# Layer 1 of a graph network: one tile in four chunks from TensorE, and weights' matmuls in 64-row pairs

## The reference, cut to what matters

```
h = relu(layernorm(x))
x = x + relu(norm_dst * segment_sum((h * norm_src)[src], dst) @ W + b)           # layer 0
h = relu(layernorm(x))                                                           # 8 scalars, 8 vectors of 3
w = relu(edge_attr_32 @ W1 + b1) @ W2 + b2      # (edges, 4, 8, 8): a weight matrix set per edge
m0 = a * ((s[src]*sh0) . w_000 + c * (v[src].sh1) . w_110)
m1 = a * (s[src] sh1 . w_011 + (v[src]*sh0) . w_101)
x = x + [segment_sum(m0) + s @ si_w0, segment_sum(m1) + v @ si_w1]               # layer 1
```

## Time and profile before

| | us |
|---|---|
| median of 3 runs | 4124.31 (4122.82 to 4134.66) |
| the profiled execution | 4122.98, span 4121.1 |
| busy: PE, PEld | 3132.6 (76%), 2298.3 (56%) |
| busy: VectorE, ScalarE | 2649.4 (64%), 1693.6 (41%) |
| busy: GpSimd | 3087.7 (75%) |
| chain of waits | GpSimd 59%, issue 24%, VectorE 8%, PE 3% |
| DMA | mean 29 GB/s |

### The profile page before, as it was taken

How to read it: one execution, slowest core, us unless ns; L and a number is a source line. 1 busy time by engine, 2 the same in 40 slices (tenths; PEclk the granted TensorE clock), 3 DMA queues, 4 the chain that set the end, 5 groups by cost and what they waited for, 6 DMA issues and landing times.

```text
span 4121.1 us, 82454 instructions
## 1 busy us (share of the span) xinstructions
PE 3132.6 (76%) x20394; PEld 2298.3 (56%) x20395; DVE 2649.4 (64%) x5843; ACT 1693.6 (41%) x5935; POOL 3087.7 (75%) x3210
## 2 busy tenths in 40 slices
PE   5654444468777777777788888888888888888887
PEld 4544444444444443343466667666677667666676
DVE  8995444455555554454577777777777777777776
ACT  3210000013333333333655555555555555555554
POOL 7767777777777777777677777777777777777775
PEclk9996555568888888988899999999999999999999
DMA  2021111111111111111111111111111111111111
GB/s 56 14 54 39 38 38 38 38 27 23 22 23 23 22 23 22 21 22 21 26 30 28 28 28 29 30 28 28 29 30 29 28 28 29 30 28 28 29 30 18
DMA packets 244961, 119.57 MB, mean 29 GB/s; under 512 B 148880, under 2 KB 226065, under 8 KB 244817
## 3 DMA queue, kind: packets, MB, share of 16 engines
q0 software_dynamic: 102528, 52.70, 9.1%
q1 hardware_dynamic: 131625, 48.99, 5.1%
q10 hardware_dynamic: 10768, 17.44, 1.3%
HBM read 113.94 MB, written 4.92 MB: 29 GB/s over the span
## 4 chain that ended last, share of the span: by engine, by line
POOL 59%; issue 24%; DVE 8%; PE 3%; DMA 1%; DVEq 1%; ACT 1%; POOLq 1%; ACTq 0%; SPq 0%
POOL g L447 59%; DVE acc_b L952 4%; DMA g<-table,idx 1%; PE ps L704 1%; PE ps L738 1%; PE ps L772 1%; ACT onehot L579 1%; DVEq L952 0%; ACT onehot L586 0%; DVE hn L1212 0%; DVE prod_a L1066 0%; DVE ef L1195 0%; ACT root L557 0%; DVE stat L905 0%; DVE stat L902 0%
## 5 line engine op out<-in xcount | busy, mean ns | idle before, releaser
L447 POOL DMA_INDIRECT g<-table,idx x2980 | 2872.1, 964 | 935.1 <-issue 902.5
L828 PE MATMUL ps<-w_s,hid 128*128 128x256 f32 x3328 | 884.8, 417 | 270.0 <-ACT hid L627 220.8
L828 PEld LDWEIGHTS ps<-w_s,hid 128*128 128x128 f32 x3328 | 660.4, 207 | 437.5 <-DVE prod_a L1270 231.3
L579 ACT ACTIVATE onehot<-iota_all,dst_rel 128x68 f32<-128x68 f32 x2648 | 673.8, 337 | 384.4 <-DVEq L1132 319.8
L639 ACT ACTIVATE q<-g,sh 128x32 f32<-128x32 f32 x1664 | 375.4, 308 | 861.5 <-DMA g<-table,idx 861.5
L738 PE MATMUL ps<-split_s,prod_a 128*128 128x512 bf16 x1736 | 572.7, 415 | 34.4 <-DVE prod_a L1057 33.5
L1275 DVE TENSOR_REDUCE msg_b<-prod_b 128x128 f32<-128x1024 f32 x416 | 502.1, 1207 | 0.0
L704 PE MATMUL ps<-onehot,g 128*33 128x68 f32 x2880 | 269.4, 263 | 273.8 <-issue 173.8
L1245 DVE TENSOR_TENSOR vsh<-g,sh 128x192 f32<-128x192 f32 x208 | 81.7, 393 | 580.1 <-ACT q L642 580.1
L704 PEld LDWEIGHTS ps<-onehot,prod_a 128*128 128x128 f32 x3328 | 388.8, 192 | 86.1 <-issue 86.0
L704 PEld LDWEIGHTS ps<-onehot,g 128*33 128x33 f32 x2880 | 233.4, 137 | 344.1 <-issue 327.5
(11 more groups left out here) (132 smaller groups left out, 3437.3 us busy)
## 6 DMA issues: line engine op xcount, KB each, us to landing
g<-table,idx POOLq DMA_INDIRECT x2980
ef<-edge_t SPq DMA_DIRECT2D x208, 128.0 KB
ef<-src_rows ACTq DMA_DIRECT2D x27, 512.0 KB, 3.6
prod_a<-src_rows SPq DMA_DIRECT2D x124, 64.0 KB, 3.0
idx<-src_chunks SPq DMA_DIRECT2D x416, 4.0 KB
g<-x_rows,idx POOLq DMA_INDIRECT x224
sh<-sh_chunks SPq DMA_DIRECT2D x208, 16.0 KB
table<-hn ACTq DMA_DIRECT2D x5, 320.0 KB, 3.5
```

The source lines that it names most:

```text
L447: pool.indirect_dma_start(out=g[:, j, t, 0:FEAT], out_offset=None, in_=table, in_offset=bass.IndirectOffsetOnAxis(ap=idx[:, j, t:t + 1], a ...
L579: ins = act.activation(onehot[:, b, t, :], iota_all[:, 0:WIN], ACT.Square, scale=-1.0, bias=dst_rel[:, bass.ds(c * TILES + t, 1)])
L828: mm = pe.matmul(w_ps[h][:, t, :], hid[:, h, P * t:P * t + P], w2_s[:, :], start=True, stop=True)
```

## The change

Layer 1 now takes tile 7 of the chunk at position 3 (ROWS_AT) of each iteration from 2 (ROWS_FROM) on from TensorE: GpSimd gathers seven tiles there. `table2` is read back in 7 groups by SP, into two stages, and split by VectorE in three bf16 parts (`split_group`), one group after each of the chunks 0 to 6. The sources of the tile are loaded into `keys2`, VectorE makes the selection at the end of step 3 (`make_source2`), TensorE multiplies in step 0 behind the window sums (`source_rows2`), VectorE chooses at the end of step 1 (`choose2`). Iterations 0 and 1 are unrolled.

Weights: both halves of `hid` lie in one buffer, half 0 in rows 0 to 63 and half 1 in rows 64 to 127, and W2 is there twice. `weights` makes both halves at once: four bf16 matmuls (32-row groups) write the bias, held as three bf16 parts in the first rows of each group of 32, into the four banks, and then the eight weight matmuls follow, half 0 and half 1 in turn, in 64-row groups, adding to it. It waits for both halves of the chunk before to be used. `hidden` writes both halves into the bank H_BANK, on partitions 0 to 63 and 64 to 127. The bank next to it takes the table's rows. ScalarE's two clears of `hid` go; a bias row is loaded and scaled, split and masked by 14 linked operations of VectorE before `weights_scaled`. SP loads three DMAs more at the start. Blocks of the output are added in `x`, not in `xc`.

```diff
--- before.py
+++ after.py
+            load_group(0)
+            load_group(1)
+            load_key2(RING * ROWS_FROM + ROWS_AT)
...
                                  load_from(sh_chunks, c + RING)).then_inc(sh_in[j], 16)
+                    if isinstance(c, int) and c + 2 < GROUPS:
+                        sp.wait_ge(split2_done, c + 1)
+                        load_group(c + 2)
+                    if j == 0 and rows_made_in(i):
+                        load_key2(RING * i + (RING + ROWS_AT))
...
                     pool.sem_inc(slots_opened, 1)
-                    for t in range(tiles):
+                    for t in range(MADE if rows_made and j == ROWS_AT else tiles):
                         pool.indirect_dma_start(
...
                 act.wait_ge(hidden_psum, 2 * (RING * i + j) + h + 1)
-                act.activation(hid[0:HID, h, :], ps[0:HID, H_BANK + h, :], ACT.Relu,
-                               bias=b1_s[:, 0:1]).then_inc(hidden_ready, 1)
+                half = slice(HID * h, HID * h + HID)
+                act.activation(hid[half, 0, :], ps[half, H_BANK, :], ACT.Relu,
+                               bias=b1_s[half, 0:1]).then_inc(hidden_ready, 1)
 
...
-                act.wait_ge(gathered[j], landed2(i))
+                act.wait_ge(gathered[j], landed2(i, j))
+                if j == ROWS_AT and rows_made_in(i):
+                    act.wait_ge(row2_made, i - 1)
...
                         row = 64 * (j % 2) + 32 * h
-                        mm = pe.matmul(ps[0:HID, H_BANK + h, at:at + 256], w1_s[row:row + 32, :],
+                        mm = pe.matmul(ps[HID * h:HID * h + HID, H_BANK, at:at + 256], w1_s[row:row + 32, :],
                                        ef[row:row + 32, 512 * (j // 2) + at:512 * (j // 2) + at + 256], start=True,
-                                       stop=True, tile_position=(row, 0))
+                                       stop=True, tile_position=(row, HID * h))
                 mm.then_inc(hidden_psum, 2)
 
-            def weights(i, j, h):
-
-                if beyond(i, j, h):
+            def weights(i, j):
+
+                if beyond(i):
                     return
-                k = 2 * (RING * i + j) + h
-                pe.wait_ge(hidden_ready, k + 1)
-                wait(pe, weights_used, k - 1)
+                k = 2 * (RING * i + j)
+                pe.wait_ge(hidden_ready, k + 2)
+                wait(pe, weights_used, k)
+                for u in range(4):
+                    h, t = u % 2, u // 2 * 2
+                    rows = slice(32 * u, 32 * u + 32)
+                    pe.matmul(w_ps[h][:, t:t + 2, :], ones_b[rows, :], bias_b[rows, :, :], start=True, stop=False,
+                              tile_position=(32 * u, 0), skip_group_check=True)
                 for t in range(4):
-                    mm = pe.matmul(w_ps[h][:, t, :], hid[:, h, P * t:P * t + P], w2_s[:, :], start=True, stop=True)
-                mm.then_inc(weights_ready, 1)
+                    for h in range(2):
+                        rows = slice(HID * h, HID * h + HID)
+                        mm = pe.matmul(w_ps[h][:, t, :], hid[rows, 0, P * t:P * t + P], w2_s[rows, :], start=False,
+                                       stop=True, tile_position=(HID * h, 0), skip_group_check=True)
+                        if t == 3:
+                            mm.then_inc(weights_ready, 1)
+
+            def source_rows2(m):
+
+                pe.wait_ge(split2_done, GROUPS)
+                pe.wait_ge(source2_ready, m + 1)
+                for k in range(GROUPS):
+                    for n in range(3):
+                        mm = pe.matmul(rows2_ps, source2[:, k, :], split[n][:, k, :],
+                                       start=(k == 0 and n == 0), stop=(k == GROUPS - 1 and n == 2))
+                mm.then_inc(rows2_psum, 1)
 
...
                     b = j % 2
-                    weights(*half(i, j, 2))
-                    weights(*half(i, j, 3))
+                    weights(i + (j + 1) // RING, (j + 1) % RING)
                     hidden(i + (j + 2) // RING, (j + 2) % RING)
                     pe.wait_ge(onehot2_ready, c + 1)
                     pe.wait_ge(messages_ready, c + 1)
                     wait(pe, added2, c - 1)
                     window_sums(c, messages_of(b), j, b, seg2_done, 1)
+                    if j == 0 and rows_made_in(i):
+                        source_rows2(i - ROWS_FROM)
                     if j == LOOK:
                         next_block(pe, blocks2, final_blocks(pe, RING * i + (LOOK - 1)), out_block)
 
...
             link(dve.tensor_scalar(w2_s[:, 64:256], w2_s[:, 64:256], float(ALPHA), None, ALU.mult))
+            dve.wait_ge(bias_in, 16)
+            link(dve.memset(ones_b, 1.0))
+            link(dve.tensor_scalar(bias_f[:, 0:64], bias_f[:, 0:64], float(ALPHA * C110), None, ALU.mult))
+            link(dve.tensor_scalar(bias_f[:, 64:256], bias_f[:, 64:256], float(ALPHA), None, ALU.mult))
+            for k in range(3):
+                link(dve.tensor_copy(bias_part, bias_f))
+                if k < 2:
+                    link(dve.tensor_tensor(bias_f, bias_f, bias_part, ALU.subtract))
+                for u in range(2):
+                    if k == 0:
+                        link(dve.tensor_scalar(bias_b[:, u, :], bias_part, masks[:, 0:1], None, ALU.mult))
+                    else:
+                        link(dve.scalar_tensor_tensor(out=bias_b[:, u, :], in0=bias_part, scalar=masks[:, k:k + 1],
+                                                      in1=bias_b[:, u, :], op0=ALU.mult, op1=ALU.add))
             dve.tensor_scalar(sel_b_s[64:96, :], sel_b_s[64:96, :], float(SI_SCALE), None,
                               ALU.mult).then_inc(weights_scaled, 1)
 
 
+            def split_group(k):
+
+                n = group_rows(k)
+                full = stage2[k % 2][0:n, :]
+                high, middle, rest = (part_s[0:n, k, :] for part_s in split)
+                dve.wait_ge(whole2_in[k % 2], 16 * (k // 2 + 1))
+                link(dve.tensor_copy(high, full))
+                link(dve.tensor_tensor(full, full, high, ALU.subtract))
+                link(dve.tensor_copy(middle, full))
+                dve.tensor_tensor(rest, full, middle, ALU.subtract).then_inc(split2_done, 1)
+
+            def make_source2(m):
+
+                dve.wait_ge(keys2_in, 16 * (m + 1))
+                dve.tensor_scalar(key2, keys2, GROUP_LOG, None, ALU.logical_shift_right).then_inc(key2_ready, 1)
+                dve.wait_ge(key2_ready, m + 1)
+                for k in range(0, GROUPS, 2):
+                    n = min(2, GROUPS - k)
+                    ins = dve.tensor_tensor(source2[:, k:k + n, :], key2[:, None, :].to_broadcast([P, n, P]),
+                                            first[:, k:k + n, None].to_broadcast([P, n, P]), ALU.is_equal)
+                ins.then_inc(source2_ready, 1)
+
+            def choose2(m, c):
+
+                dve.wait_ge(rows2_psum, m + 1)
+                dve.scalar_tensor_tensor(
+                    out=chosen2.rearrange("p f b -> p b f"),
+                    in0=iota_all[:, 0:GROUP, None].to_broadcast([P, GROUP, FEAT]), scalar=low[:, bass.ds(c, 1)],
+                    in1=rows2_ps.rearrange("p (b f) -> p b f", f=FEAT),
+                    op0=ALU.is_equal, op1=ALU.mult).then_inc(chosen2_ready, 1)
+                dve.wait_ge(chosen2_ready, m + 1)
+                dve.tensor_reduce(g[:, ROWS_AT, MADE, 0:FEAT], chosen2, AX, ALU.add).then_inc(row2_made, 1)
+
             def d_coefs(i, j):
 
                 c = RING * i + j
                 b = j % 2
+                if j == ROWS_AT and rows_made_in(i):
+                    dve.wait_ge(row2_made, i - 1)
                 dve.wait_ge(coefs_ready, c + 1)
...
                         products(c + 1, nxt[1], 0)
+                    if isinstance(c, int) and c < GROUPS:
+                        split_group(c)
+                    if j == ROWS_AT - 2 and rows_made_in(i):
+                        choose2(i - ROWS_FROM, RING * i + ROWS_AT)
+                    if j == ROWS_AT and not (isinstance(i, int) and not ROWS_FROM - 1 <= i < ITERS - 1):
```

More of the change, by code:

```diff
@@ L74 @@
 MADE = TILES - 1
+ROWS_FROM = 2
+ROWS_AT = RING - 1
 M_ALL = RING * (REG_ITERS - A_ITERS)
@@ L262, in over_iterations, with over_layer2, rows_made_in @@
             body(ITERS - 1)
+        def over_layer2(eng, body):
+            for i in range(ROWS_FROM):
+                body(i)
+            with eng.Fori(ROWS_FROM, ITERS - 1) as i:
+                body(i)
+            body(ITERS - 1)
+        def rows_made_in(i):
+            return not isinstance(i, int) or i >= ROWS_FROM
         def final_blocks(eng, c):
@@ L304, in gnn_program, with group_rows @@
         mid_ps = ps[:, W_BANK, 0:BR * (FEAT + 1)].rearrange("p (r f) -> p r f", f=FEAT + 1)
+        stage2 = [flat_hn[:, (2 + k) * BLOCK:(3 + k) * BLOCK] for k in range(2)]
+        chosen2 = flat_hn[:, 4 * BLOCK:5 * BLOCK].rearrange("p (f b) -> p f b", b=GROUP)
```

(28 more changed lines are left out.)

73 lines of the change are left out of this document (48 added, 25 removed).

## The result

The changed kernel takes 4249.43 us, the median of 4 runs (4241.06 to 4278.52), against 4124.4 before: ratio 1.031 on record (of the medians alone 1.030), interval 1.029 to 1.034. It is 125 us slower, where I forecast 58 faster. The profiled execution took 4253.46, its span 4251.6.

A forecast was written before the change was run, and what follows sets the result against it. GpSimd's gathers were taken as the bound, before and after: 4123.0 less 62.9 for 50 fewer gathers plus 5 for backlog at the end gives 4065, or 4066 against the median; range 4057 to 4112.

The forecast's parts named there:

- What goes: Layer 1, GpSimd: 50 gathers fewer at 1.259 us each, 62.9 us saved; its round becomes 39.0 us.
- What VectorE gets: Layer 1, VectorE: choose 1.8 and selection 1.6 us a round, table split about 2.8 in chunks 0 to 6.
- The price of the pairs: Layer 1, TensorE: paired weights take 2.7 us a chunk instead of 3.65.
- rival 2: Layer 1, TensorE: pairs don't run side by side, weights 4.2 us, round 44.9, time 4366; 0.10, including what lies toward rival 1.
- the 1.7 among my signs: Sign of being wrong: hidden layer of 1.7 us on TensorE, from both halves lying in one PSUM bank.
- The round in series: Layer 1 with VectorE backlog: TensorE and VectorE take 37.3 us a round at full clock, output blocks add 0.7.
- the part of the round that is TensorE's: Layer 1's round: 19.5 us are TensorE's and lose 0.9 at clock 0.957; sum 38.9 against GpSimd's 39.0.
- rival 1: Layer 1: TensorE and VectorE in series become the pace, round 39.7 to 40.1, time 4078 to 4130; chance 0.26.
- Start and end: Layer 1: backlog 9 us at first, 11 at chunk 7, then shrinking; 5 us left behind the last gather.
- GpSimd isn't held: Start of layer 1: the backlog doesn't hold GpSimd; of 24 us before it needs the buffer, 13 are left.
- VectorE without a wait for q: Sign of being wrong (rival 1): VectorE waits for weights in every round and never for ScalarE's q.
- a clock under 0.93: Sign of being wrong: TensorE's granted clock falls under 0.93.

The follow-up runs named there:

- both steps moved: Changed kernel with `choose2` and `make_source2` moved ahead of half 0's products in step 1; 4071.8 us, ratio 0.9865 against the kernel before.
- the pairs alone: Changed kernel with paired weights kept but no rows made, eight tiles gathered in every chunk; 4123.56 us, ratio 0.9999 against the kernel before.

## Why the prediction was wrong

It failed in one term of the round, the clock's, and what hangs on it.

1. *What goes*: right. 2930 gathers, 964 ns each, as before. With both steps moved 57 of the 62.9 us appear (4128.8 to 4071.8).
2. *What VectorE gets*: choose 1.80, selection 1.55, a split group 2.4, near what I priced (1.8, 1.6, 2.8). Left out: 0.85 and 0.66 us of issue behind choose and selection, about 1.5 a round.
3. *The price of the pairs*: right kind, a little dear. At full clock, from the bias's load at 3013.67 to the next group at 3015.95, it is 2.28 us, forecast 2.7. No run shows the parts that the 2.7 was added up from, nor those put on top of 3.65 in rival 2's 4.2; they were estimates of mine. What the traces show is this. Before, L828's passes start 0.216 apart (2035.72 to 2038.53, 13 steps), and from the first to the next group are 3.65 (2035.19 to 2038.84). After, L899's start in twos, under 0.01 apart, with 0.216 from one two to the next (3014.35 to 3015.64, 6 steps): from the first to the next group 1.92 (3014.03 to 3015.95), and 0.36 for the bias ahead of it. The 21 table matmuls start 0.216 apart too (1419.25 to 1423.57). Rival 2 is out. The hidden layer in one bank takes 1.08, the next group 1.01 after its start, as with two; no run showed the 1.7 among my signs.
4. *The round in series*: right, in part by luck. 37.3 at full clock plus 0.7 for output blocks is 38.0 (1.3 in 25 of 52 rounds is 0.6, a slip). The kernel with useless matmuls took 37.7 at clock 1.00 without a block. A straight line through the 42 rounds after, against their clock, is 38.0 + 28 x (1/clock - 1). That dear pairs (4 x 0.4 too much) and left-out issue (1.5 too little) nearly cancel is the luck.
5. **The step that failed**: "the part of the round that is TensorE's is 11.4 + 3 x 2.7 = 19.5; at 0.957 it loses 0.9". I carried over a clock measured while TensorE had long work and waits of at most 2.3 us, though my own order gave it a new wait in every chunk. The clock was 0.867, and the round lost 4.4 us against the 38.0 at full clock, not 0.9. Most of that can be counted without the line: two sets of weights a round at about 3.53 instead of 2.00 are 3.1, their bias matmuls at 0.61 instead of 0.40 are 0.4, and the hidden layer (1.23 for 1.08 on average) and window sums (3.21 for 3.07) add some. The line splits the same loss as 28 x 0.156 = 4.4. It was fitted to these very rounds, so it is a description of them and no test, and it doesn't carry over: the rounds of the kernel with three table matmuls give a slope of 17, those with `choose2` moved 37. With 19.5 and the clock as measured, my term would have been 3.0 and the round 41.0: the clock was the larger error, the part of the round that it acts on the smaller. The round is 42.4, 3.4 above the gathers' 39.0, and 50 x 3.4 = 170 us turn -62.9 into +107. I had rival 1 as this mechanism, but with a clock of 0.92 and a range that ended at 4130, and put the gathers first by a margin of 0.1 us in 39. Rival 1 also named the half clock behind output blocks, but the sum left it out; here it is 20 of the 85 slow sets of weights. Of my chances only the 0.10 for rival 2 and what lies between it and rival 1 reached 4249, and rival 2 isn't what came.
6. *Start and end*: "GpSimd isn't held" was wrong. With the clock at 0.73, chunks 1 to 7 begin 11.8 to 12.6 us apart, where I had 10.3. GpSimd waits for VectorE's q at 2080.96 (1.26 us), and 8 us in all before 2200. That alone costs nothing: the pairs alone have the same slow start (12.0 to 12.6 us) and the time of the kernel before. But here the round stays above the gathers', so the backlog never shrinks: 23.5 us more than before at the end, where I took 5 (11 in rival 1).

Of the signs I named, VectorE without a wait for q and a clock under 0.93 came. GpSimd stood idle too, but behind the indices' load and only once behind VectorE's q.

## What to carry to other kernels

The clock of a stretch can't be carried over: from 2200 to 4000 it was 0.96 before, 0.87 in the change, 0.81 with three table matmuls and 0.98 with useless ones. Where a change shortens TensorE's work and puts it in series with another engine, price the round with the weights at 2.00 us and at the 3.5 us that they took here behind the long waits, before calling it hidden. Work for VectorE that frees nobody belongs behind the operation that TensorE waits for, or where TensorE has its own work to do: the same two steps at another place of the same loop were worth 178 us. And a margin of 0.1 in 39 us is a tie: then the sign hangs on the least known term.

## What the runs showed of the hardware

- 21 matmuls a round whose result nobody uses made the kernel 137 us faster (4249.4 to 4112.5) and raised layer 1's clock from 0.87 to 0.98.
- Removing work lowered the clock twice: the pairs alone took it from 0.96 to 0.83, 18 matmuls fewer a round from 0.87 to 0.81.
- In the change each of the 65 sets of weights behind TensorE's waits of 3.0 to 3.6 us took 2.94 to 3.79 us instead of 2.00, and the 20 right behind an output block, without a wait, took 3.23 to 3.79.
- float32 matmuls of 64 rows in two row groups overlap: 16 passes in 2.00 us, 0.125 each, against 3.72 for 16 of 128 rows. Four bf16 matmuls of 512 columns in 32-row groups took 0.40 together.
